# Bulk loads and stores on a second queue: mixing weights and mixed halves issued by GpSimd in a one-core Fourier-layer kernel

## The reference

```python
x1 = spectral_conv(h, w1, w2)                       # rfft2, 2 x 12 x 12 modes mixed over channels, irfft2
x2 = einsum('bchw,oc->bohw', h, conv_w[i]) + conv_b[i]
h  = layer_norm(x1 + x2, ln_g[i], ln_b[i])          # then gelu, in all layers but the last
```

## Time and profile before

| | |
|---|---|
| median of three runs | 3360.97 us |
| the profiled execution, its own time | 3361.34 us |
| its span in the trace | 3359.6 us |
| mean granted PE clock | 0.956 |
| PE busy | 2941.6 us, 88% of the span |
| DVE busy | 2141.6 us, 64% |
| ACT busy | 1948.0 us, 58% |
| POOL busy | 29.1 us, 1%, 17 instructions |
| data DMA queues in use | one (SP's), 333.48 MB, 30.8% of 16 engines |

### The profile page before, as it was taken

The page is one execution under the profiler, slowest core; times in us unless marked ns, Lnnn a source line. Parts: engine busy times, 40 slices in busy tenths (PEclk is TensorE's granted clock), DMA queues, the critical chain, the costliest instruction groups (busy, mean ns, idle before and its releaser), DMA issues.

```text
span 3359.6 us, 82075 instructions
## 1 busy us (share of the span) xinstructions
PE 2941.6 (88%) x32240; PEld 1871.7 (56%) x32240; DVE 2141.6 (64%) x3949; ACT 1948.0 (58%) x2271; POOL 29.1 (1%) x17
## 2 busy tenths in 40 slices
PE   3888897999887999887999879999999987973994
PEld 2545465666665666655666644444444447961893
DVE  3888775888665888666888644444544444246457
ACT  3777664666554666554666547777777753432451
POOL 0000000000000000000000010000000001000000
PEclk7999999999998999999999999999999997996897
DMA  5222156444447444447444443111111000000000
GB/s 95 95 97 95 70 190 191 162 166 166 129 159 202 164 161 160 140 146 205 164 167 164 155 108 85 57 44 44 57 53 57 29 1 1 1 1 0 1 1 13
DMA packets 114157, 335.91 MB, mean 100 GB/s; under 512 B 45993, under 2 KB 78025, under 8 KB 78153
## 3 DMA queue, kind: packets, MB, share of 16 engines
q1 hardware_dynamic: 113992, 333.48, 30.8%
HBM read 179.29 MB, written 154.14 MB: 99 GB/s over the span
## 4 chain that ended last, share of the span: by engine, by line
PE 75%; DVE 10%; issue 5%; ACT 4%; SPq 3%; DMA 2%; DVEq 0%; ACTq 0%
PE pA L1286 14%; PE pA L1294 7%; PE pT L1380 7%; PE pT L1312 4%; PE pS L1323 4%; PE pD L1369 4%; PE pD L1337 4%; PE pD L1351 4%; PE pD L466 3%; PE pA L466 3%; PE pA L1276 2%; PE pD L1258 2%; DMA h_scratch<-h_new 2%; PE pS L458 2%; PE pT L458 2%
## 5 line engine op out<-in xcount | busy, mean ns | idle before, releaser
L1607 DVE TENSOR_REDUCE small<-arena 128x32 f32<-128x1056 f32 x320 | 396.8, 1240 | 353.4 <-ACT arena L1456 347.2
L1286 PEld LDWEIGHTS pA<-conv_bd,h_in 128*128 128x128 f32 x4096 | 478.8, 192 | 109.4 <-issue 92.7
L1286 PE MATMUL pA<-conv_bd,h_in 128*128 128x128 f32 x4096 | 517.1, 280 | 8.6 <-DVE arena L1600 3.0
L1446 ACT COPY w_sb<-pA 128x1024 f32<-128x1024 f32 x256 | 259.7, 1015 | 382.9 <-PE pA L1294 333.5
L1467 ACT ACTIVATE h_new<-pT,bet,gam 128x1024 f32<-128x1024 f32 x256 | 307.3, 1201 | 157.2 <-PE pT L1312 92.5
L1621 DVE SCALAR_TENSOR_TENSOR w_sb<-w_sb,small 128x1024 f32<-128x1024 f32 x320 | 386.6, 1212 | 5.5
L1456 ACT ACTIVATE arena<-w_sb 128x1024 f32<-128x1024 f32 x320 | 339.3, 1060 | 13.6
L1312 PE MATMUL pT<-cst,w_sb 128*128 128x128 f32 x2048 | 285.4, 284 | 64.1 <-ACT h_new L1467 43.0
L1312 PEld LDWEIGHTS pT<-cst,w_sb 128*128 128x128 f32 x2048 | 227.3, 144 | 185.5 <-issue 167.2
L1471 ACT COPY h_rows<-pS 128x1024 f32<-128x1024 f32 x256 | 256.9, 1004 | 66.1 <-PE pS L1323 66.1
L1323 PEld LDWEIGHTS pS<-cst,h_new 128*128 128x128 f32 x2048 | 228.8, 143 | 113.7 <-issue 71.9
(11 more groups left out here) (292 smaller groups left out, 3866.6 us busy)
## 6 DMA issues: line engine op xcount, KB each, us to landing
h_scratch<-h_new SPq DMA_DIRECT2D x128, 1024.0 KB, 4.2
h_in<-h_scratch SPq DMA_DIRECT2D x128, 1024.0 KB, 5.0
y_scratch<-w_sb SPq DMA_DIRECT2D x32, 576.0 KB, 8.8
y_in<-y_scratch SPq DMA_DIRECT2D x512, 36.0 KB
w_sb<-in_L_tok_w1r_dram SPq DMA_DIRECT2D x8, 576.0 KB, 11.5
w_sb<-in_L_tok_w1i_dram SPq DMA_DIRECT2D x8, 576.0 KB, 11.3
w_sb<-in_L_tok_w2r_dram SPq DMA_DIRECT2D x8, 576.0 KB, 18.0
w_sb<-in_L_tok_w2i_dram SPq DMA_DIRECT2D x8, 576.0 KB, 18.2
```

The lines of the kernel that those rows point to most:

```text
L1286: pe.matmul(pA[:, c:c + 128], h_in[:, 1024 * n + c:1024 * n + c + 128], conv_bd[:], start=(j == 0), stop=False, skip_group_check=True)
L1607: dve.reduce_sum(var[n], sq[n % 2], axis=AX).then_inc(s["summed"], 1)
```

## The change

The 8 DMAs of `weights(L)` and the 4 of `y_store` leave SP's program and are issued by GpSimd, in the order in which it waits for them anyway; the weights' order is now first all of slot 0, then slot 1. `conv_w` is read in 4 DMAs by rows of 128 bytes, turned by one transpose on VectorE and put in place by 4 copies. `conv_params` is now the `then` of group 0; `mlp_params` comes after group 1; `token_params` comes after group 1 of the last phase, where it came after group 0. The list of semaphores, which gains `conv_turned`, and the bodies of the two functions that only moved are left out:

```diff
--- before.py
+++ after.py
@@ -269,6 +269,7 @@
         TA = V.rearrange("p (h b c q) -> p b h c q", h=2, b=2, q=NQ)
         XF = [arena[:, 5152 + 768 * t:5920 + 768 * t] for t in range(2)]
         conv_all = arena[:, 7744:8256]
+        conv_rows, conv_cols = w_sb[:, 13312:13440], w_sb[:, 13440:13568]
         cbias = arena[0:C, 8256:8384]
         mlp = arena[:, 8384:8648]
         h_in = sb("h_in", [P, 4096])
@@ -357,7 +358,7 @@
...
@@ -1004,22 +1005,11 @@
                 sp.wait_ge(s["h_new_ok"], at("h_new", ph, L, g, 2 * t + 2))
                 sp.dma_start(h_dram[g][:, c], h_new[:, c]).then_inc(s[f"stored{t}"], 16)
 
-            def weights(L):
...
-
             def conv_params():
+                for j in range(4):
+                    sp.dma_start(conv_rows[32 * j:32 * j + 32, :].rearrange("p (l c) -> p l c", l=LAYERS),
+                                 ins["L0_tok_conv_w"].rearrange("l o c -> o l c")).then_inc(s["conv_loaded"], 16)
                 sp.wait_ge(s["conv_cleared"], 1)
-                for L in range(LAYERS):
-                    for j in range(4):
-                        c = P * L + 32 * j
-                        sp.dma_start(conv_all[32 * j:32 * j + 32, c:c + 32],
-                                     ins["L0_tok_conv_w"][L].rearrange("o c -> c o")).then_inc(s["conv_loaded"], 16)
                 sp.dma_start(cbias, ins["L0_tok_conv_b"].rearrange("l o -> (l o)").partition_broadcast(C)).then_inc(s["conv_loaded"], 16)
 
             def mlp_params():
@@ -1035,22 +1025,6 @@
                     for k in range(2):
                         sp.dma_start(fc3_pad[q, k, 2 * k + j:2 * k + j + 1], ins["L0_tok_fc3_w"]).then_inc(s["mlp_loaded"], 16)
                 sp.dma_start(fc3_b, ins["L0_tok_fc3_b"].partition_broadcast(P)).then_inc(s["mlp_loaded"], 16)
-
-            def y_store(L, half):
...
             def y_is_stored(L, half):
                 sp.wait_ge(s["y_stored"], 64 * (2 * L + half) + 64)
@@ -1120,33 +1094,27 @@
 
             def groups(ph, L):
 
-                def second_half():
-
-                    y_store(L, 1)
-                    weights(L + 1)
-
-                group(ph, L, 1, second_half if ph == "mid" else None)
+                group(ph, L, 1)
                 if ph == "mid":
                     y_is_stored(L, 1)
-                with sp.Fori(2, NG - 2) as g:
+                else:
+                    mlp_params()
+                with sp.Fori(2, NG - 1) as g:
                     group(ph, L, g)
-                group(ph, L, NG - 2, lambda: y_store(0 if ph == "first" else L + 1, 0))
                 group(ph, L, NG - 1)
 
-            weights(0)
-            conv_params()
-            mlp_params()
             sp.wait_ge(s["y_clear"], 1)
-            group("first", 0, 0)
+            group("first", 0, 0, conv_params)
             groups("first", 0)
             with sp.Fori(0, LAYERS - 1) as L:
                 group("mid", L, 0)
                 groups("mid", L)
             L = LAYERS - 1
-            group("last", L, 0, lambda: y_store(L, 1))
+            group("last", L, 0)
+            group("last", L, 1)
             y_is_stored(L, 1)
             token_params()
-            with sp.Fori(1, NG - 1) as g:
+            with sp.Fori(2, NG - 1) as g:
                 group("last", L, g)
             sp.wait_ge(s["acc_done"], 1)
             sp.dma_start(out_ap.rearrange("(t b) y x -> (b y) t x", b=2), X.rearrange("p (t x) -> p t x", x=S)).then_inc(s["out_stored"], 16)
@@ -1157,12 +1125,39 @@
         def _(pool):
             pool.memset(arena[:, 7744:8384], 0.0).then_inc(s["conv_cleared"], 1)
             pool.memset(mlp, 0.0).then_inc(s["mlp_cleared"], 1)
+
+            def weights(L):
+                for slot in range(2):
+                    for w, (wr, wi) in enumerate((("L0_tok_w1r", "L0_tok_w1i"), ("L0_tok_w2r", "L0_tok_w2i"))):
+                        for r in range(2):
+                            q = slice(64 * w + 32 * r, 64 * w + 32 * r + 32)
+                            pool.dma_start(w_v[q, slot].rearrange("p o m -> p (o m)"),
+                                           ins[wr if slot == r else wi][L].rearrange("i o x y -> i (o x y)")).then_inc(s["w_loaded"], 16)
+
+            def y_store(L, half):
+
+                n = 2 * L + half
+                pool.wait_ge(s["y_bias"], n + 1)
+                pool.wait_ge(s["mix_a_free"], 3 * n + 3)
+                pool.wait_ge(s["mix_b_free"], 3 * n + 3)
+                for p in range(2):
+                    for xh in range(2):
+                        q = 64 * p + 32 * xh
+                        dst = y_dram.rearrange("b (p w n) -> p b w n", p=2, w=2)[p][32 * half:32 * half + 32, :, 2304 * xh:2304 * xh + 2304]
+                        src = w_sb[q:q + 32, 13312:17920].rearrange("b (w n) -> b w n", w=2)
+                        pool.dma_start(dst, src).then_inc(s["y_stored"], 16)
+
+            weights(0)
             for L in range(LAYERS):
+                y_store(L, 0)
                 if L == 0:
                     pool.wait_ge(s["conv_chain"], 2)
                 else:
                     pool.wait_ge(s["acc_full"], at("acc", "mid", L, 0, 0))
                 pool.tensor_copy(conv_bd[:], conv_all[:, P * L:P * L + P]).then_inc(s["conv_ready"], 1)
+                y_store(L, 1)
+                if L < LAYERS - 1:
+                    weights(L + 1)
             pool.wait_ge(s["mix_a_full"], 6 * LAYERS)
             pool.wait_ge(s["mix_b_full"], 6 * LAYERS)
             pool.memset(spec[:, 0:at_col[0]], 0.0).then_inc(s["par_cleared"], 1)
@@ -1533,7 +1528,15 @@
 
             def conv_centre():
 
-                dve.wait_ge(s["conv_loaded"], 16 * 17)
+                dve.wait_ge(s["conv_loaded"], 16 * 5)
+                dve.transpose(conv_cols, conv_rows).then_inc(s["conv_turned"], 1)
+                dve.wait_ge(s["conv_turned"], 1)
+                dve.wait_ge(s["conv_cleared"], 1)
+                for j in range(4):
+                    q = slice(32 * j, 32 * j + 32)
+                    dve.tensor_copy(conv_all[q].rearrange("p (l c) -> p l c", l=LAYERS)[:, :, 32 * j:32 * j + 32],
+                                    conv_cols[q].rearrange("p (l o) -> p l o", l=LAYERS)).then_inc(s["conv_turned"], 1)
+                dve.wait_ge(s["conv_turned"], 5)
                 cv, cb = conv_all.rearrange("p (x o) -> p x o", o=C), cbias.rearrange("p (l o) -> p l o", o=C)
                 dve.reduce_sum(cv_sum, cv, axis=AX)
                 dve.reduce_sum(cb_sum, cb, axis=AX).then_inc(s["conv_chain"], 1)
```

22 lines of the change are left out of this document (1 added, 21 removed).

## The result

The changed kernel takes 3340.69 us, the median of seven executions (3336.29 to 3347.9), against 3360.97 for the kernel before. The ratio is 0.9946, with a 95% interval of 0.993 to 0.9963: 18 us faster, 12 to 24. The profiled execution took 3339.68, its span is 3337.9 (before 3361.34 and 3359.6) and the mean granted clock 0.962 (0.956). The spans differ by 21.7 us where the sum said 34.6. Medians and ratios of the experiments leave out executions that ran over 4% longer at a lower granted clock: two of six of i1_best and two of four of h1_one_queue_unsplit, whose other two times stand in place of a median.

The account below looks back on a forecast made before the run. The prediction blamed 76 us of DMA stalls on SP's queue order, with full engines in the middle. Terms 35.3 - 14.5 - 1.2 + 15 = 34.6 off 3361.3 gave 3326 on the median's scale; 8-in-10 range 3280 to 3342.

Parts of the forecast that it names:

- its own case: Whole kernel: 3326 us, range 3312 to 3342, start losing 8 to 20, middle giving 0 to 8 a layer; chance 0.52.
- turns by rows: Start and middle: engines alternate between queues, so each small load waits behind one weight row of 1.43 us.
- Gain 35.3 at most: Start: x of group 1 is issued at 18.5, removing the 33.05 us wait and 2.2 of slow clock.
- I take the upper end, 14.5: Start: fc0 loads wait behind weight rows on GpSimd's queue, the last landing at 27 instead of 12.2; 14.5 us lost.
- DVE's turn of the channel weights, 1.2: Between bodies 1 and 2: one transpose and four copies on DVE lose at most 1.2 us.
- `mlp_params`, half 0, `conv_bd` at 0: Moved parameter loads, half-0 stores and the conv_bd copy all have slack before use, so they cost 0.
- The last phase at 0: Last phase: token_params moves behind group 1, y_in of group 3 queued behind it is read later; cost 0.
- rival C: GpSimd hands y_store's descriptors over late, seven times; slower if over 10.7 us late, 3384 at 14; chance 0.05.
- Middle: I take 5.0; three layers, 15.: Middle: h_new's stall goes, but y_in waits behind weight rows; body 3 starts at 557, gaining 5.0 per layer.
- A: Start and middle: SP's small transfers are not held up by the other queue's weights; 3285 us, chance 0.2.
- B: Start and middle: the other queue cuts its rows, so turns are shorter than a weight row; 3308 us, chance 0.17.
- D: Start: weights begin late, at 12 or more, delaying norm loads and x; half the start is won, 3345, chance 0.06.

Follow-up runs that it names:

- i1_best: g3_one_queue's order on SP, but weights on GpSimd in two parts, the first ones held until fc0 and norm loads land; 3280.57 us, ratio 0.9782.
- h1_one_queue_unsplit: g3_one_queue with the next layer's weights whole again, all eight loads behind group 1 on SP's queue; its two times are 3317.54 and 3327.3 us.
- f1_hold_start: Changed kernel, but GpSimd waits for the fc0 and norm loads to land before issuing the first weights; 3319.53 us, ratio 0.9886.
- g4_old_channel_loads: f1_hold_start with the 16 transposed channel-weight loads put back, behind x of group 1; 3328.39 us, ratio 0.9909.
- f4_quarter_rows: Changed kernel with each weight load cut into four, rows of 4608 bytes instead of 18432, same bytes; 3334.17 us, ratio 0.9923.
- f3_no_weights_mid: Changed kernel without the weight loads of layers 1 to 3, which mix with layer 0's weights centred again; 3295.38 us, ratio 0.9813.
- g1_two_parts: Changed kernel with the next layer's weights in two parts, slot 0 where it was, slot 1 behind y_in of group 5; 3308.02 us, ratio 0.9858.
- g3_one_queue: Changed kernel with no GpSimd DMA in the layers: all on SP's queue, reordered, later layers' weights split by slot; 3289.84 us, ratio 0.9807.

## Why the prediction went wrong

It forecast 3326, with its own case from 3312 to 3342; 3340.69 came. The direction, the two places and both mechanisms were right: turns by rows at the start, and a middle where the stall is handed from `h_new` to `y_in` while full engines carry the same bytes. The size was too large: 34.6 us, where the profiled spans show 21.7 and the ratio 18. At 3340.69 the time is inside the stated range, but at its slow end. The terms, in their order:

- **"Gain 35.3 at most", x of group 1.** The wait of 33.05 is gone whole. Of the 2.2 for the clock behind it 1.8 came, if what group 2 gained beyond group 1 is put down to it: the transform of group 2 stands at 71.41 instead of 87.97, 16.6 earlier, that of group 1 14.75 earlier.
- **"I take the upper end, 14.5", the weights beside `fc0`.** By the prediction's own terms (27 less 12.2) it was 14.8. Nearer 19 came: the last weight row ends at 27.05, as forecast, but the chain ends 16.7 later than before (28.87), and behind the longer wait four more matmuls ran at twice their length, 3.76 instead of 1.98, 1.8 us, and the first four lost 0.35. The sum had no term for what PE runs at behind the new wait.
- **DVE's turn of the channel weights, 1.2.** 1.4 (16.56 earlier at group 2, 15.2 at group 3), and 2.6 in f1_hold_start. What the term left out is on the other side: the rows free SP for 29 us, which is worth some 6 (g4_old_channel_loads); in the sum it had no place of its own, since all of it was put down to x.
- **Start in all.** 15.3 where 35.3 - 14.5 - 1.2 = 19.6 was forecast, 4.3 short. The measured terms add up to 14.6 and leave 0.7 open.
- **`mlp_params`, half 0, `conv_bd` at 0.** Nothing in the profile speaks against it: x of group 3 is read 15.2 earlier like all behind it.
- **The last phase at 0.** It lost 3.3. The forecast looked at SP's queue only; `y_store(3, 1)`, which it also leaves out of rival C's count of seven (there are eight), is now issued ahead of GpSimd's clearing, and that holds up DVE. Luck behind the last group (3.8) covers it in the span.
- **"Middle: I take 5.0; three layers, 15." This is the step that failed.** Body 3 was to start 5.0 earlier, at 557, with PE waiting about 10 us for `y_in`. Measured from the start of body 2, it starts 38.49 behind it instead of 43.55, 5.06 earlier, and PE waits 10.12 us: the first half of the step held to a tenth. But the step stopped there. Of the kernel before I had counted the slow clock behind the gap as removed; it lay inside body 2 and so inside the 5.0. After the change the gap stands at the head of body 3, and the slow clock behind it (0.57) makes body 3 last 30.71 instead of 27.63. That gives back 3.1 of the 5.1: the moved gap was charged with its wait and not with the slow clock behind it. (DVE's centring found its weights, as the step says: 546.94, without a wait.) In the other two layers body 3 starts 4.7 and 3.7 earlier after body 2, lasts 2.9 and 1.8 longer, and 1.9 is won each (17.3 to 15.4, 16.5 to 14.6). Three middles won 5.8, not 15. The 5.1 came nearly as said, but the premise behind it, the same bytes in the same time, did not hold: the weights' rows took the engines 17.3 us instead of 21.4, and 1.97 MB of `h` moved beside them before `y_in` was there, where the forecast had one store. That the two came out at 5.1 together is in part luck.

Of the rivals, A (small transfers pass unhindered) is refuted at both places by the waits of 24.6 and 10.12. B (turns shorter than a row) is refuted for 18 KB rows, which the other queue does not cut: each is one transfer; f4_quarter_rows shows that with quartered rows it would have been right at the start and worthless in the middle. C, slower, did not come: GpSimd issues `y_store` within 2.08 us of the end of the mix and the weights at 0.49 to 0.66 us per DMA, and PE waits after that for `y_in`, which was issued by SP. The issues from 506.64 to 507.87 ran beside a 1.23 us operation of DVE from SBUF to SBUF in fp32 and kept their 0.49 us. The Trainium skill's warning ("SBUF — State Buffer", the box on DVE blocking DMA) concerns copies in a faster mode; nothing of it shows here. D's amount, half of the start, came nearest of all in microseconds, but by another way: the weights started at 1.59, not late.

The larger miss is one of view. I took the bytes of the middle as given and asked only who waits for them. f3_no_weights_mid shows that the whole excess hangs on the weights in that stretch, g1_two_parts that half of them needn't be there, and g3_one_queue that the new queue isn't needed for most of what can be won.

## What to carry to other kernels

When a stall comes from full DMA engines, a second queue moved the stall here and shortened it little; ask instead which bytes needn't move in that stretch, and split a bulk load by when its parts are first read. Before bulk rows go on a second queue, list the small loads of the other queue that something waits for in that time, and charge each of them the time of up to one bulk row. And where a gap is moved rather than removed, count what PE runs at behind it in its new place as well. When DMAs move into another engine's program, look at what that engine does behind them, and who waits for it.
